# Seeding the sums of the last pass from ScalarE, and the first layer of the last block in the summed layout

## The reference

```python
w = einsum('bpf,mf->bpm', features, W_ft) + b_ft     # 1024 x 2 x 512, inner length 5128
l1_x = clip(stm * w, 0.0, 1.0).reshape(1024, -1)     # 1024 x 1024
l2_x = clip(l1_x @ W1.T + b1, 0.0, 1.0)              # 1024 x 32
out  = l2_x @ W2.T + b2                              # 1024 x 1
```

## Time and profile before

| | us |
|---|---|
| median of 3 runs | 411.7 |
| lowest and highest run | 410.91, 411.74 |
| the profiled execution, its own time | 409.96 |
| span of the profiled execution | 408.2 |
| TensorE (PE) busy | 398.5 |
| VectorE (DVE) busy | 349.1 |
| ScalarE (ACT) busy | 191.4 |
| mean granted TensorE clock, share of 2.4 GHz | 0.997 |

### The profile page before, as it was taken

The page is one execution under the profiler, slowest core; times in us unless marked ns, Lnnn a source line. Parts: engine busy times, 40 slices in busy tenths (PEclk is TensorE's granted clock), DMA queues, the critical chain, the costliest instruction groups (busy, mean ns, idle before and its releaser), DMA issues.

```text
span 408.2 us, 4646 instructions
## 1 busy us (share of the span) xinstructions
PE 398.5 (98%) x1764; PEld 322.6 (79%) x1764; DVE 349.1 (86%) x331; ACT 191.4 (47%) x182; POOL 12.7 (3%) x32
## 2 busy tenths in 40 slices
PE   8999799999999999999999999999999999999995
PEld 5778688888888888888888888888888888888851
DVE  3999999899999999999984889999888755996335
ACT  4465644644474444444444854444444457444200
POOL 1000009000000000000000000000000000000000
PEclk9999999999999999999999999999999999999998
DMA  7999788987666777676506799876676777771000
GB/s 232 400 397 399 275 257 233 346 287 266 235 245 232 254 259 251 210 253 232 213 4 255 243 361 332 323 274 246 254 259 206 245 228 222 237 220 60 2 0 0
DMA packets 30182, 96.39 MB, mean 236 GB/s; under 512 B 3752, under 2 KB 9648, under 8 KB 24912
## 3 DMA queue, kind: packets, MB, share of 16 engines
q1 hardware_dynamic: 29536, 95.44, 67.7%
q0 software_dynamic: 624, 0.66, 0.8%
HBM read 96.08 MB, written 0.00 MB: 235 GB/s over the span
## 4 chain that ended last, share of the span: by engine, by line
PE 87%; DVE 7%; issue 2%; DMA 1%; ACT 1%; SPq 0%; DVEq 0%
PE sums L555 85%; DVE xs L417 2%; DMA open_x<-x_p 1%; DVE x_lo_home L394 1%; DVE x_lo_early L394 1%; ACT x_hi L315 1%; DVE ws L407 1%; PE sums L617 1%; PE sums L661 1%; DVE w_lo L389 1%; DVE x_lo_home L443 1%; DVE ws L421 0%; DVE c_early L536 0%; DVE c_early L540 0%; ACT x_hi L304 0%
## 5 line engine op out<-in xcount | busy, mean ns | idle before, releaser
L555 PE MATMUL sums<-x_hi,w_hi 128*128 128x512 f32 x560 | 175.0, 392 | 1.5 <-ACT x_hi L298 0.9
L555 PE MATMUL sums<-x_hi,w_lo 128*128 128x512 f32 x560 | 174.0, 391 | 0.0
L555 PEld LDWEIGHTS sums<-x_hi,w_hi 128*128 128x128 f32 x560 | 105.2, 189 | 26.2 <-ACT x_hi L315 1.4
L329 ACT ACTIVATE x_hi<-xs 128x2048 fp32r<-128x2048 f32 x64 | 122.1, 1908 | 3.9 <-DVE xs L434 3.0
L555 PEld LDWEIGHTS sums<-x_hi,w_lo 128*128 128x128 f32 x560 | 105.7, 189 | 22.2
L555 PE MATMUL sums<-x_lo_home,w_hi 128*128 128x512 f32 x384 | 119.1, 390 | 2.2 <-DVE x_lo_home L443 2.2
L324 ACT ACTIVATE w_hi<-ws 128x512 fp32r<-128x512 f32 x64 | 40.6, 635 | 169.4 <-PE sums L555 165.7
L443 DVE TENSOR_TENSOR x_lo_home<-xs,x_hi 128x2048 fp32r<-128x2048 f32 x44 | 100.6, 2287 | 6.7 <-ACT x_hi L329 6.6
L555 PEld LDWEIGHTS sums<-x_lo_home,w_hi 128*128 128x128 f32 x384 | 72.2, 188 | 17.7 <-issue 2.6
L440 DVE TENSOR_TENSOR w_lo<-ws,w_hi 128x512 fp32r<-128x512 f32 x64 | 43.9, 686 | 11.4 <-ACT w_hi L324 11.4
L427 DVE TENSOR_TENSOR xs<-xs 128x2048 f32<-128x2048 f32 x20 | 45.7, 2283 | 0.0
(11 more groups left out here) (74 smaller groups left out, 150.7 us busy)
## 6 DMA issues: line engine op xcount, KB each, us to landing
xs<-x_p SPq DMA_DIRECT2D x40, 1024.0 KB, 5.6
xs<-x_p SPq DMA_DIRECT2D x57, 512.0 KB, 6.7
ws<-w_p SPq DMA_DIRECT2D x57, 256.0 KB, 3.5
ws<-w_p SPq DMA_DIRECT2D x43, 128.0 KB, 4.6
open_x<-x_p SPq DMA_DIRECT2D x2, 512.0 KB, 6.6
stm_all<-stm SPq DMA_DIRECT2D x1, 1024.0 KB, 8.3
open_x<-x_p SPq DMA_DIRECT2D x2, 256.0 KB, 4.0
open_w<-w_p SPq DMA_DIRECT2D x3, 128.0 KB, 4.4
```

The lines of the kernel that those rows point to most:

```text
L329: nc.scalar.activation(x_hi[:, g % HI, :, :], x_pair(g), ACT.Copy).then_inc(x_hi_ready, 1)
L555: return nc.tensor.matmul(sums[:, bank, :], w[:, m * P:(m + 1) * P], x[:, c * BANK:(c + 1) * BANK], start=start, stop=stop, skip_group_che ...
```

## The change

Four edits:

1. In the third drain ScalarE writes P1 plus the bias of output part m into each of banks 0 to 3, once that bank is drained (`seed(b)`, 128x512 from SBUF to PSUM). It does so for bank b behind the drain of bank b + 1. TensorE's last pass waits for the seed of a bank instead of its drain, and does not clear the bank, so that its products sum onto the seed.
2. VectorE's work on a finished bank of block 0 is two instructions: times 1.0 times `stm` out of PSUM, and the clip.
3. The first layer of block 0 no longer goes through the four-contribution bank. For each bank b, four matmuls of 128 columns put the contribution of bank b of each group of 128 positions straight onto its quadrant of bank 7, in the summed layout (`first_layer_of_bank`). `add_halves` of half 0, which now carries only block 2, stands behind bank 1 and opens the sum there.
4. TensorE's order: bank 0's first-layer group stands behind bank 2; behind bank 3 come bank 1's group, the second layer of half 1, and the groups of banks 2 and 3.

```diff
+            def seed(b):
+                sc.wait_ge(drained, 16 + b + 1)
+                nc.scalar.activation(sums[:, b, :], c_all[0][:, b * BANK:(b + 1) * BANK], ACT.Identity,
+                                     bias=b_ft_col[:, b // 2:b // 2 + 1]).then_inc(seeded, 1)
...
                         nc.scalar.activation(to, src, ACT.Identity, bias=b_ft_col[:, m:m + 1])\
                             .then_inc(drained, 1)
+                        if 1 <= b <= 4:
+                            seed(b - 1)
...
                 dve.wait_ge(bank_full, 7 * PASSES + b + 1)
-                nc.vector.scalar_tensor_tensor(out=c_all[0][:, cols], in0=sums[:, b, :],
-                                               scalar=b_ft_col[:, b // 2:b // 2 + 1], in1=c_all[0][:, cols],
-                                               op0=ALU.add, op1=ALU.add).then_inc(last_sum, 1)
-                dve.wait_ge(last_sum, 2 * b + 1)
-                nc.vector.tensor_tensor(c_all[0][:, cols], c_all[0][:, cols],
-                                        stm_all[:, 0, (b % 2) * BANK:(b % 2 + 1) * BANK], ALU.mult)\
-                    .then_inc(last_sum, 1)
-                dve.wait_ge(last_sum, 2 * b + 2)
+                nc.vector.scalar_tensor_tensor(out=c_all[0][:, cols], in0=sums[:, b, :], scalar=1.0,
+                                               in1=stm_all[:, 0, (b % 2) * BANK:(b % 2 + 1) * BANK],
+                                               op0=ALU.mult, op1=ALU.mult).then_inc(last_sum, 1)
+                dve.wait_ge(last_sum, b + 1)
...
-                    start = first and (f == 0 or f == PASSES or (f == 1 and bank == 4))
+                    start = first and (f == 0 or (f == 1 and bank == 4))
...
                             if first:
-                                pe.wait_ge(drained, 8 * (f - 1) + b + 1)
+                                if f < PASSES:
+                                    pe.wait_ge(drained, 8 * (f - 1) + b + 1)
+                                else:
+                                    pe.wait_ge(seeded, b + 1)
...
                         if b == 0:
-                            add_halves(0, 1)
+                            add_halves(0, 1, True)
+                        if b == 1:
+                            add_halves(1, 0, False)
                         if b == 2:
-                            second_layer(0, 1)
+                            first_layer_of_bank(0)
+                first_layer_of_bank(1)
+                second_layer(0, 1)
+                first_layer_of_bank(2)
+                first_layer_of_bank(3).then_inc(l1_summed, 1)
+                second_layer(1, 0)
...
+            def first_layer_of_bank(b):
+                m, c = divmod(b, PERSP)
+                pe.wait_ge(act_ready, 3 + b + 1)
+                for q in range(Q):
+                    mm = nc.tensor.matmul(sums[q * L1:(q + 1) * L1, 7, 0:QB], w1_sb[:, c * UT + m, :],
+                                          c_all[0][:, b * BANK + q * QB:b * BANK + (q + 1) * QB],
+                                          start=False, stop=b == 3, skip_group_check=True)
+                return mm
```

More of the change, by code:

```diff
@@ L138, in feature_net @@
         drained = sem("drained")
+        seeded = sem("seeded")
         idle_zeroed = sem("idle_zeroed")
@@ L664, in first_layer, with add_halves @@
                 return mm
-            def add_halves(n, h):
+            def first_layer_of_bank(b):
[6 more added lines that the diff above has]
+                return mm
+            def add_halves(n, h, whole):
                 pe.wait_ge(part_ready, n + 1)
@@ L669, in add_halves @@
                     mm = nc.tensor.matmul(sums[q * L1:(q + 1) * L1, 6 + n, 0:QB], add_up[:, :],
-                                          part[:, h, q * QB:(q + 1) * QB], start=True, stop=True)
-                mm.then_inc(l1_summed, 1)
+                                          part[:, h, q * QB:(q + 1) * QB], start=True, stop=whole,
+                                          skip_group_check=True)
+                if whole:
+                    mm.then_inc(l1_summed, 1)
             def second_layer(n, h):
@@ L694, in _ @@
             pe.wait_ge(act_ready, 3)
-            first_layer(1, 0, 2, 1, True, False)
+            first_layer(1, 0, 2, 1, True, True).then_inc(l1_full, 1)
             closing()
[L697 to L706, removed]
 def kernel(**inputs):
```

## The result

Over all runs on the chips that ran both, the changed kernel takes 408.33 us (407.09 to 408.96, 7 runs), the kernel before 410.91 (409.77 to 411.74, 7 runs). The ratio is 0.9936, 95% interval 0.9914 to 0.9957: faster by 2.6 us (1.8 to 3.5). The profiled execution took 407.09 us with a span of 405.3; before, 409.96 and 408.2.

The account below looks back on a forecast made before the run. TensorE bounds the kernel, busy 398.5 of 408.2 us, with a serial chain of waits at the end. Terms 0.72 + 1.83 + 0.10 + 0.2 = 2.85 us off 411.7 give 408.9 us, range 407.8 to 410.4.

Parts of the forecast that it names:

- (a): Tail, VectorE: two instructions for a bank instead of three, the multiply L540 goes; gain 0.72 us.
- (b): Tail after the clip: one group of four small matmuls, then VectorE, replaces the path through ScalarE; gain 1.83 us.
- The rival in which the four quadrant groups run one after another: Closing groups: eight weight loads in series, 0.86 us instead of 0.35; 1.7 of 2.85 gone, 410.5 us; chance 0.07.
- (c): Ahead of bank 3's last product: two small groups add 1.12 us, the second layer's leaving saves 1.23; gain 0.10.
- (d): Last second-layer product: runs at the high clock, 2.4 GHz, instead of 1.2; gain 0.2 us, 0 if already down.
- What could come late: Behind bank 3's last product: TensorE's three small pieces take 1.34 us, VectorE's way 1.70, so TensorE is free 0.36 earlier.
- The seeds: Third drain, ScalarE: four seeds of 0.62 us each, bank 3's over by 341.6, no TensorE stall; cost 0.
- The formula for the stall: TensorE, start of last pass: stall of 4s - 3.13 us for a seed of s us, starting at s = 0.78.
- rivals 2 and 3: Seeds of 1.2 us stall TensorE 1.7 us (chance 0.05); seeds of 1.90 us stall it 4.5 us, time 413.3 (0.03).
- Up to 389 us it waits for nothing: Kernel before the change: TensorE, busy for 398.5 of 408.2 us, has no waits until the tail.
- Rival 4: Gain absent: something unnamed binds the tail, or the start falls out otherwise by 1 to 2 us; about 411.3; chance 0.06.

Follow-up runs that it names:

- the filled tail: Kernel before plus five idle 256-column bfloat16 matmuls behind block 0's first-layer products, where TensorE waits for ScalarE: 409.83 us, ratio 0.9992.
- without small groups: Changed kernel with the other half's adding-up ahead of the closing steps, second adding-up and bank 0's group behind bank 3: 406.84 us, ratio 0.9905.

## Why the prediction was right

**The terms.** Forecast 2.85 us, in the profile 2.88. The four terms are the four differences that the profile shows.

- (a) The multiply: 0.72 forecast, 0.78 measured. I had left VectorE's first instruction at 0.75; with a constant for its scalar it takes 0.69. The run with a scalar from memory and the one without seeds both show it.
- (b) From 2.32 to 0.49: exactly so (402.03 to 402.52). The rival in which the four quadrant groups run one after another is out: the group has the length of L669, 0.43, and 1.02 us of detour.
- (c) 0.10 forecast, 0.06 measured at bank 3's last product. The size held, and the accounting was of the right kind, but it hid something that I could have read: of the 1.23 us taken out, 0.72 were a wait for VectorE's three instructions. The seeds alone remove it (0.63 us instead of 1.35 from bank 2's last product to the next), and beside bank 0's group the second layer costs only 0.15 there. Credit for the wait belongs as much to edit 2 as to edit 4, and so does that for the clock of term (d). The terms were summed for all edits together, so the sum did not suffer; a forecast for the seeds by themselves from term (a) would have been off by 0.94.
- (d) 0.2 forecast, 0.21 measured between these two profiles, cause shown by the filled tail. It is not gained in every execution, since the clock did not fall in every run of the kernel before.

**What could come late.** TensorE's small pieces end 1.17 us after bank 3's last product; I had 1.34, because I gave each piece what it takes between banks (0.35 a group, 0.31 the second layer), where part is the return to the large products: behind bank 3 the next small piece starts 0.25 us after a group (400.71 to 400.96). The rule of the Trainium skill that I weighed ("TensorE: Matmul & The Clock Gate", section Back-to-back issue gap: about 81 ns for a 128-column matmul with its weights) does not fit this form, counted by records: eight of them with their weights take 0.35 us ahead of a large product, after as before, and 0.23 to 0.25 ahead of another small piece.

**The seeds.** 0.62 assumed, about 0.61 to the next instruction; last seed over by 341.3 against 341.6 forecast; roundings 1.5 us late against 1.9; no stall. The formula for the stall was tried with doubled seeds: 4s - 3.13 gives 2.27 for 1.35 us (the expectation of that run, worked out from an end at 344.1, has 2.0), measured 2.04. It is high by the drains, which follow each other and the seeds by 0.57 us here and not by 0.62. So rivals 2 and 3 were priced rightly to 0.2 us and did not occur.

**A reading that was wrong.** "Up to 389 us it waits for nothing" does not hold for the kernel before. Its trace has

```profile
44.45 0.70 PE L555 MATMUL sums<-x_lo_home,w_hi 128*128 128x512 f32 x2 [2.18 <-DVE x_lo_home L443]
```

and TensorE is busy for 55.28 of the first 60 us. The change moves nothing there, so the gain did not suffer, but the scatter of the runs that the prediction left open begins at this row.

**The median.** 408.9 forecast, 408.33 measured. The difference comes from what the gain was taken from: the median of the first three runs was 411.7, that of all seven is 410.91. Less 2.85 that is 408.06, 0.27 under the measured time. By the medians the gain is 2.58, by the ratio 2.6 (1.8 to 3.5), so the agreement of 2.85 with 2.88 is one of two profiles that happened to start their closing part at the same time; the runs alone would not have told 2.85 from 2.0. Rival 4, in which the start falls out otherwise, is real as a scatter, though not as an effect of the change.

## What to carry to other kernels

Where the end of a kernel is a chain with nothing beside it, price it by start-to-start steps of the rows, and put small work of another kind behind the last large product, where the next engine's latency covers it, not between large products. A wait that two edits both remove may be credited to either only once: run each edit alone before saying what it is worth. And an accumulator that lies idle (here a bank that the matmuls of the pass before had filled completely; no run tried another) can be seeded by an engine that has time long before the end, if the seed is priced against the first use of its bank and not against the average load of the engine.

## What the hardware showed that I had not expected

**Most of the scatter of the runs comes from a fall of TensorE's clock, near 45 us.** The runs of a kernel lie 1.2 to 3.4 us apart, and in the two profiles of the changed kernel the closing part starts at 389.72 and at 391.21, 1.5 us later. In the seventh step of the first pass TensorE waits for the first low part of a full step. The row of that wait, in the second profile of the changed kernel:

```profile
44.31 0.70 PE L559 MATMUL sums<-x_lo_home,w_hi 128*128 128x512 f32 x2 [2.19 <-DVE x_lo_home L451]
```

The granted clock around it, in the same profile (stretch, length, busy PE, PEld, DVE, ACT, POOL, clock, DMA):

```profile
44.00:46.00 2.00, 1.69 (x6) 1.46 (x7) 2.00 (x5) 0.97 (x2) 0.00 (x0) 0.83 1.05 366
46.00:48.00 2.00, 2.00 (x6) 1.54 (x6) 2.00 (x2) 1.58 (x1) 0.00 (x0) 0.50 0.94 375
```

The clock falls to 0.50 (1.2 GHz) behind the wait; between 48 and 50 us it is 0.82, and from 50 us on 1.00 again. In the first profile of the changed kernel, with the same wait (2.17 us), it stays up:

```profile
46.00:48.00 2.00, 2.00 (x11) 1.65 (x10) 2.00 (x3) 1.75 (x1) 0.00 (x0) 1.00 0.95 378
```

The eleven profiles of kernels without this filling divide the same way: where the clock between 46 and 48 us is 0.50 to 0.58 (six), the block of first-layer products starts at 390.9 to 391.4, or at 393.2 with doubled seeds and their stall; where it is 1.00 (five), at 389.5 to 390.1. In the version with 16 matmuls of zeros in the place of the wait:

```profile
42.15 1.92 PE L635 MATMUL sums<-idle 128*128 128x256 bf16 x16
44.48 0.70 PE L559 MATMUL sums<-x_lo_home,w_hi 128*128 128x512 f32 x2 [0.41 <-DVE x_lo_home L451]
```

TensorE idles only 0.41 us, the clock stays up, and the runs lie within 0.42 us of each other. The filling is worth 1.1 to 1.4 us, about half as much as the whole change: by the ratios to the kernel before beside each, 0.9936 to 0.9908 for the changed kernel and 0.9905 to 0.9870 without small groups. That the runs of other kernels differ by more than 1.5 us is not accounted for by the profiles, of which each kernel has one or two; in the nine runs with the filling none of that is left either. Products of zeros suffice to hold the clock here. Why the clock falls in one execution and not in the next, with waits of the same length, no run tells.

**A matmul group of four output quadrants.** Four 32-column matmuls of 128 columns, with their eight weight loads of 0.108 us, take 0.23 to 0.25 us up to the start of the next small piece (400.71 to 400.96 in the changed kernel, two groups in 0.46 with bank 0's group behind), and 0.35 where a large product follows. Eight loads one after another would take 0.86, so they overlap. The two records of a 4-column second layer slip in between (400.96 in the rows above). Between large products a group costs 0.56 to 0.61, so more than half of that lies at its two edges: it starts 0.32 us behind a large product instead of 0.23 (398.20 to 398.52), the product behind it comes some 0.1 us late, and the step after that is 0.34 instead of 0.23.
